# GpSimd builds half of a one-hot matmul operand in the slot inversions of a two-layer attention and expert kernel

## The reference

```python
x = x + _L0_xattn_ref(_layernorm(x, axis=-1), ctx_1024, ctx_1024, mask_BxS2_bf0, ...)
x = x + _L0_ffn_ref(_layernorm(x, axis=-1), ...)   # E = 32, K = 4
x = x + _L1_xattn_ref(_layernorm(x, axis=-1), ctx_1024, ctx_1024, ...)
x = x + _L1_ffn_ref(_layernorm(x, axis=-1), ...)   # NUM_EXPERTS = 8, TOP_K = 2
...
vals, idx = jax.lax.top_k(gf, K)
```

## Time and profile before

| | us |
|---|---|
| median of 3 runs | 1754.67 (1753.66 to 1758.85) |
| the profiled execution, its own time | 1755.46 |
| its span, first to last instruction | 1753.6 |
| inversion of the first layer, first compare to `token_of_slot` | 386.6 to 456.5 |
| inversion of the second layer, first compare to `token_of_slot` | 1327.8 to 1360.8 |

### The profile page before, as it was taken

The page is one execution under the profiler, slowest core; times in us unless marked ns, Lnnn a source line. Parts: engine busy times, 40 slices in busy tenths (PEclk is TensorE's granted clock), DMA queues, the critical chain, the costliest instruction groups (busy, mean ns, idle before and its releaser), DMA issues. The chain is left out here.

```text
span 1753.6 us, 56922 instructions
## 1 busy us (share of the span) xinstructions
PE 1360.9 (78%) x20300; PEld 1058.5 (60%) x20303; DVE 1170.2 (67%) x3429; ACT 956.9 (55%) x2354; POOL 1117.1 (64%) x1400
## 2 busy tenths in 40 slices
PE   5999999739677777776368788887854799999784
PEld 3677777514477667676246666665632588777663
DVE  5788888689577777776358888888869222322265
ACT  2677777627445555454156777776735344444332
POOL 3777777500477777775477778887410677777773
PEclk8999999969899999998669999999985899999988
DMA  4211111000144444447233222222100112112284
GB/s 164 85 45 36 45 36 46 21 7 1 33 107 108 103 108 106 105 109 83 69 92 125 64 62 63 63 63 60 36 17 1 49 54 55 54 53 54 55 216 150
DMA packets 136994, 122.85 MB, mean 70 GB/s; under 512 B 27675, under 2 KB 121915, under 8 KB 136123
## 3 DMA queue, kind: packets, MB, share of 16 engines
q0 software_dynamic: 26624, 56.35, 14.1%
q1 hardware_dynamic: 110078, 64.47, 12.1%
q10 hardware_dynamic: 192, 0.67, 0.1%
HBM read 80.24 MB, written 41.18 MB: 69 GB/s over the span
## 5 line engine op out<-in xcount | busy, mean ns | idle before, releaser
L1501 POOL DMA_INDIRECT arena<-expert_rows,token_of_slot x432 | 416.8, 965 | 281.7 <-issue 220.2
L419 POOL DMA_INDIRECT arena<-slot_results,slot x256 | 250.3, 978 | 104.5 <-issue 69.1
L1892 DVE TENSOR_TENSOR arena<-bank,arena 128x352 f32<-128x352 f32 x144 | 75.5, 524 | 223.1 <-ACT arena L1871 220.8
L1825 PE MATMUL bank<-W,arena 128*128 x576 | 196.8, 465 | 0.9 <-ACT arena L1883 0.9
L1736 POOL DMA_INDIRECT token_results<-arena,slot x144 | 141.1, 980 | 53.3 <-issue 41.4
L728 ACT ACTIVATE arena<-bank 128x512 f32<-128x512 f32 x256 | 132.1, 603 | 71.9 <-PE bank L910 59.2
L596 DVE TENSOR_REDUCE mx<-bank 128x8 f32<-128x512 f32 x256 | 158.4, 681 | 15.5 <-PE bank L873 12.6
L445 POOL TENSOR_TENSOR arena<-arena,fixed 128x1024 f32<-128x1024 f32 x64 | 121.3, 1916 | 46.0 <-ACT arena L746 46.0
L1599 PE MATMUL bank<-arena 128*128 128x128 f32 x1152 | 148.4, 285 | 0.0
L1599 PEld LDWEIGHTS bank<-arena 128*128 128x128 f32 x1152 | 141.5, 200 | 0.2
L1839 PEld LDWEIGHTS bank<-W,arena 128*128 128x128 f32 (+1 forms) x864 | 115.1, 192 | 37.9 <-issue 30.5
(11 more groups left out here) (215 smaller groups left out, 3349.8 us busy)
## 6 DMA issues: line engine op xcount, KB each, us to landing
slot_results<-arena SPq DMA_DIRECT2D x72, 256.0 KB, 2.5
arena<-in_ctx SPq DMA_DIRECT2D x64, 128.0 KB
expert_rows<-arena SPq DMA_DIRECT2D x64, 128.0 KB, 1.9
arena<-token_results SPq DMA_DIRECT2D x32, 256.0 KB, 4.1
arena<-expert_rows,token_of_slot POOLq DMA_INDIRECT x432, 2.6
W<-in_w SPq DMA_DIRECT2D x4, 1032.0 KB
X<-in_x SPq DMA_DIRECT2D x32, 128.0 KB, 2.2
arena<-slot_results,slot POOLq DMA_INDIRECT x256
```

Of the source, the lines that this page charges most:

```text
L419: nc.gpsimd.indirect_dma_start(out=gb[i.par][:, to:to + D], out_offset=None, in_=ys, in_offset=bass.IndirectOffsetOnAxis(ap=slot[:, at, k: ...
L1501: nc.gpsimd.indirect_dma_start(out=XE[n % R][:, c * ROW:(c + 1) * ROW], out_offset=None, in_=ts, in_offset=bass.IndirectOffsetOnAxis(ap=to ...
L1825: last = nc.tensor.matmul(H_[2 * r + u][:, 0:F1], XT[i.par][:, c * P:(c + 1) * P], W1a[:, bass.ds(x_e, 1), u * F1:(u + 1) * F1], start=Tru ...
```

## The change

For the second tile of each pair the low part no longer goes through DVE and ACT. GpSimd makes that half of `by_id` itself, with one `tensor_scalar` for each choice: it compares the ramp (128 fp16 numbers, read with a step of K elements) with the token's low part and multiplies by its `ids`, both scalars being one fp32 number per partition. That is K operations of 128 elements for a pair, and a new semaphore `scaled_odd` that PE waits on too. DVE's low compare then covers one tile (half as many elements), ACT runs one activation for a pair instead of two, and DVE makes a copy of the low parts as fp32, `low_f`, once for each layer. The high compare, the matmuls and their operands are as they were.

```diff
@@ -1292,7 +1292,7 @@
                         sp.dma_start(ts_rows[:, :, D:ROW], pay[:]).then_inc(weights_out, 16)
 
         hots_high, hots_low = sem("hots_high"), sem("hots_low")
-        scaled = sem("scaled")
+        scaled, scaled_odd = sem("scaled"), sem("scaled_odd")
         summed = sem("summed")
         split = sem("split")
 
@@ -1310,7 +1310,8 @@
             iota_s, ids, unused = inverse_iotas(K, NT)
             high_i, low_i = carve(TILES * K, I32), carve(TILES * K, I32)
             high, low = carve(TILES * K, F16), carve(TILES * K, F16)
-            hot_low, by_id, hot_high = ([carve(2 * K * w, F16) for _ in range(3)] for w in (P, P, NT))
+            low_f = carve(TILES * K)
+            hot_low, by_id, hot_high = ([carve(K * w, F16) for _ in range(3)] for w in (P, 2 * P, 2 * NT))
             offset, found = carve(NT), carve(NT)
             in_quarter, second = carve(NT), carve(NT)
             total = bank[0:4]
@@ -1328,6 +1329,22 @@
                         sp.wait_ge(b_in, 80)
 
                         sp.wait_ge(expert_in, 128)
+
+                @block.gpsimd
+                def _(pool):
+                    pool.wait_ge(split, 2 * layer + 2)
+                    for n in range(PAIRS):
+                        if n >= 3:
+
+                            pool.wait_ge(summed, n + base - 2)
+                        for k in range(K):
+                            i = 2 * n + 1
+                            at = (K + k) * P
+                            last = nc.gpsimd.tensor_scalar(
+                                by_id[n % 3][:, at:at + P], iota_s[:, 0:P * K].rearrange("p (s k) -> p s k", k=K)[:, :, 0],
+                                low_f[:, i * K + k:i * K + k + 1], ids[:, i % QUARTER:i % QUARTER + 1],
+                                ALU.is_equal, ALU.mult)
+                        last.then_inc(scaled_odd, 1)
 
                 @block.vector
                 def _(dve):
@@ -1336,6 +1353,7 @@
                                             ).then_inc(split, 1)
                     dve.wait_ge(split, 2 * layer + 1)
                     nc.vector.tensor_copy(high, high_i)
+                    nc.vector.tensor_copy(low_f, low_i)
                     nc.vector.tensor_copy(low, low_i).then_inc(split, 1)
                     dve.wait_ge(split, 2 * layer + 2)
 
@@ -1366,12 +1384,12 @@
                         if n >= 3:
 
                             dve.wait_ge(summed, n + base - 2)
-                        for part, w, hot, done in ((low, P, hot_low, hots_low), (high, NT, hot_high, hots_high)):
+                        for part, w, of, hot, done in ((low, P, 1, hot_low, hots_low), (high, NT, 2, hot_high, hots_high)):
                             nc.vector.tensor_tensor(
-                                hot[c].rearrange("p (i s k) -> p i s k", i=2, k=K),
+                                hot[c].rearrange("p (i s k) -> p i s k", i=of, k=K),
                                 iota_s[:, 0:w * K].rearrange("p (s k) -> p s k", k=K).unsqueeze(1)
-                                .broadcast_to([P, 2, w, K]),
-                                ik(part)[:, 2 * n:2 * n + 2, :].unsqueeze(2).broadcast_to([P, 2, w, K]),
+                                .broadcast_to([P, of, w, K]),
+                                ik(part)[:, 2 * n:2 * n + of, :].unsqueeze(2).broadcast_to([P, of, w, K]),
                                 ALU.is_equal).then_inc(done, 1)
                         if layer and n > QUARTER // 2 and n % (QUARTER // 2) == 1:
                             add_quarter(n // (QUARTER // 2) - 1)
@@ -1408,13 +1426,10 @@
                         if n >= 3:
 
                             act.wait_ge(summed, n + base - 2)
-                        for j in range(2):
-                            at = (2 * n + j) % QUARTER
-                            last = nc.scalar.activation(
-                                by_id[c].rearrange("p (i k s) -> p i k s", i=2, k=K)[:, j, :, :],
-                                hot_low[c].rearrange("p (i s k) -> p i k s", i=2, k=K)[:, j, :, :], ACT.Copy,
-                                scale=ids[:, at:at + 1])
-                        last.then_inc(scaled, 1)
+                        at = 2 * n % QUARTER
+                        nc.scalar.activation(by_id[c][:, 0:K * P].rearrange("p (k s) -> p k s", k=K),
+                                             hot_low[c].rearrange("p (s k) -> p k s", k=K), ACT.Copy,
+                                             scale=ids[:, at:at + 1]).then_inc(scaled, 1)
 
                 @block.tensor
                 def _(pe):
@@ -1423,6 +1438,7 @@
                         g, in_g = n // (QUARTER // 2), n % (QUARTER // 2)
                         pe.wait_ge(hots_high, n + base + 1)
                         pe.wait_ge(scaled, n + base + 1)
+                        pe.wait_ge(scaled_odd, n + base + 1)
                         for j in range(2):
                             for k in range(K):
                                 of_k = k if layer else 0
```

## The result

The changed kernel is **slower by 5.6%**: 1854.78 us median (1852.49 to 1860.92) beside 1757.03 us (1753.66 to 1758.85) of the kernel before, six runs each; ratio 1.0561 [1.055, 1.0572]. The forecast was 1801 us, range 1757 to 1850. The direction was right, and in the main the mechanism; the size was not: +98 us instead of +46.

What follows compares the result with a forecast made beforehand. PE was taken to bound the first inversion, ACT the second; GpSimd's operations and collisions add +36.7 and +12.9 us, hidden additions -3, the fp32 copy +0.4, together +47 us: 1801 us, range 1757 to 1850.

Steps and rivals of the forecast that it cites:

- The bound before: First inversion: PE bounds at 2.05 us a pair, DVE 0.2 us behind; second: ACT bounds at 0.80 to 0.81 us.
- c: Time of one new GpSimd operation of 128 elements in the inversions: 0.35, 0.48 or 0.87 us, with 0.48 taken.
- the prediction's own sum: Both inversions: GpSimd's operations plus DVE's compares less 0.25 us dispatch behind each compare; 3.20 and 1.20 us a pair.
- less 3 and plus 0.4 us: Second inversion's quarter additions become largely hidden, -3 us; the fp32 copy on DVE ahead of both layers' loops, +0.4 us.
- the third rival: GpSimd's operation is heavy, 0.6 to 0.9 us, by step or two scalars; with the lock 1825 to 1882 us; chance 0.14.
- the lock: In both loops DVE and GpSimd do not read SBUF side by side; the second waits for the other's whole operation.
- The first rival: The lock holds, but GpSimd's operation is light, 0.35 to 0.42 us: around 1777 us; chance 0.20.
- The second rival: No lock for fp16 compares, each engine at its own pace: 1757 us unchanged (chance 0.09) or 1749 us faster (0.07).
- They alternate: In the loops DVE and GpSimd take turns, so their times add up, less 0.25 us dispatch behind each compare.
- The additions of a quarter: Second inversion: three additions leave gaps costing some 4 us; under pairs already compared, some 3 us come back.
- The wait on `scaled_odd`: First inversion: PE waits on GpSimd, holding up the pair's other seven matmuls and `summed`; 3.20 us a pair against 2.05.

Runs made afterwards that it cites:

- at c = 0.497: Kernel before plus, in the first layer, four GpSimd compares with a constant per pair into scratch, which PE waits for: 1792.36 us (one run).
- at a third of the price: Kernel before plus, in the first layer, four GpSimd additions with multiplication by constants per pair into scratch, which PE waits for: 1777.19 us (one run).

## Why the prediction was wrong, and where it was right

**The bound before** was read rightly: PE at 2.05 us for a pair, DVE 0.2 us behind, savings on DVE and ACT worth nothing. The kernel with `hot_high` in pairs of choices bears it out: with PE made faster, the pair takes DVE's 1.87 us. No run took the saved work away by itself. (The 15 compares of the earlier trace rows end where that view ends; by the single instructions DVE made 20 before it first waited. The 1.87 us stand.)

**The step that failed is the price of GpSimd's operation.** The prediction bounded c between 0.35 and 0.87 us and took 0.48, by the row that it held to be nearest, a tensor_tensor at 1.87 ns for an element. Measured are 0.778 us and 3.5 ns for an element, with 0.33 us fixed where 0.25 was taken. The row that was put aside, L1153 at about 5 ns, gave 0.87 us and was nearer, but that was luck. L1153 is a single addition of a constant; the same on 128 elements with a step of 8 bytes lasts 536 ns, by the same reckoning (536 - 220) / 126 = 2.5 ns for an element, half of L1153's. So L1153 has a cost of its own, perhaps its long step, as the prediction supposed; in the change's operation the step costs next to nothing (0.778 and 0.773 us). What sets this operation above the light addition with multiplication stood in no row of before: a compare in front of the multiplication (0.35 us more than an addition there, though alone the two cost the same) and two scalars per partition (0.17 us). Why the first of these costs so much stays open. "Reading the two scalars can only add" was in the text, and no number was given to it.

With c = 0.778 the prediction's own sum gives 4 x 0.778 + 1.775 - 0.5 = 4.39 us for a pair of the first layer (+75 us) and 2 x 0.778 + 0.741 - 0.5 = 1.80 us in the second (+32 us), less 3 and plus 0.4 us, in all +104 us or 1859 us; 1854.78 was measured. The stretches gave +71.9 and +26.4 us. So the error, +98 us instead of +46, is in the main this one term, which stands in the sum 4 x 32 and 2 x 32 times: 192 operations by 0.298 us are 57 us.

**Which case it was.** It was the third rival, the heavy operation with the lock, at 1825 to 1882 us, which had a chance of 0.14. Of its two reasons one fell (the step), the other is a part (the scalars). The first rival's light operation exists, at 0.26 us for an addition and multiplication by constants, but it isn't this one. The Trainium skill ("GPSIMD Engine Reference", 3.1 Elementwise) states some 1.03 cycles for an element of a body of at most two operations, by which the estimate was 0.36 us; the 0.778 us measured here contradict that for a compare and multiply, the 0.261 us of the addition and multiplication lie below it.

**The second rival, no lock for fp16 compares**, is excluded: with one of the compares' inputs moved to PSUM, all of GpSimd's waiting is gone (104 operations in 80.00 us instead of 110.00), though DVE is busy for longer. The Trainium skill's rule ("SBUF — State Buffer", Who interferes with whom), that a DVE instruction with two SBUF inputs and a GpSimd instruction that reads SBUF exclude each other, agrees with these rows. What the same page of the Trainium skill says under "SBUF: two separate sides", that the loser is blocked for the other's whole instruction, is borne out here for GpSimd as the loser, but not for DVE: DVE lost 0.1 us to a GpSimd operation of 0.5 us, and at most 0.23 us (0.65 instead of 0.42) to one of 0.78 us. In the earlier trace rows DVE did lose 1.6 us (2.01 instead of 0.425) to GpSimd operations of 2.03 us with two inputs each; so what DVE loses depends on GpSimd's operation, and rows of one kind did not price the other.

**"They alternate"** was therefore too simple. What the lock costs a pair of the first layer was put at 1.775 - 0.5 = 1.28 us; measured are 1.17 us (4.28 less 3.11, from pair distances of 3.11 and 5.45 us in turn). The size was right, the account was not: GpSimd pays nearly all of it, for whole high compares, while DVE has the time to run two pairs of compares one soon after the other and then wait. So that the size came out at c = 0.778 is partly luck: how much two such streams cost each other hangs on how they fall together, and at c = 0.497 the same account was 0.4 us too high.

**The smaller terms.** The additions of a quarter in the second layer cost 4.0 us before (pair distances of 1.49, 2.44 and 2.43 us instead of 0.80); after, the longest distance is 2.32 us where others are 1.55 to 2.01, so they are largely hidden, as forecast. The second inversion lost 26.4 us where the sum with the measured c has 29. The wait on `scaled_odd` did what was said: PE's whole idle time ends with GpSimd's line.

Put together, of the +71.9 us of the first layer about 34 us are GpSimd's own pace (32 pairs by 3.11 - 2.05 us) and about 37 us the lock (32 by 1.17 us); taking away the lock there gave back 36 us. Neither alone would do: without the lock the four operations are still longer than PE's pair, and at a third of the price, with the full low compare beside it, the pair is still 0.5 us longer than PE's.

## What to carry to other kernels

Work handed to an idle engine is only free if that engine's chain, collisions included, is shorter than the pace of the engine that bounds the loop; here it took 4c plus 1.1 to 1.5 us against 2.05 us, so c had to be below 0.24 us at best, and the cheapest form that does arithmetic took 0.26. Where the trace of before has no operation of the same kind, the price stands for the whole sum: keep the dear bound alive in the range, even where the row that supports it is dear for a reason of its own. And what bounded the loop was the operand that PE reads with a step: half that step gave 3 us, where the rearranged work of three engines cost 98.

## What the runs showed of the hardware

- On GpSimd an addition of a constant alone takes longer than an addition with a multiplication behind it: 0.498 us against 0.261 us, for the same 128 elements. With a compare it is the other way round: a compare alone takes 0.497 us, compare and multiplication 0.611 us. Why is open; no run here looked into the operation.
- A matmul of 288 columns whose moving operand has a step of 8 bytes starts every 0.256 us, at a granted clock of 0.50 (1.2 GHz, the kernel after, PE waiting on GpSimd between the pairs) as at 1.00 (2.4 GHz, the kernel before, PE without a break). With a step of 4 bytes, at 1.00, it is 0.127 us. So the kernel after lost nothing by the lower clock in its matmuls, and the kernel before was held by the operand's step, not by the clock.
- DVE's fused compare and multiply of 128 fp16 elements starts every 0.223 us, against 0.778 us on GpSimd.
